# Graph network, four layers: writing the x columns of the wide node rows by DRAM to DRAM transfers ahead of the first node stage

## The reference, cut to what matters

```python
h = jnp.maximum(_layernorm(x), 0.0)
h = h @ W                                   # 128 x 128
deg = segment_sum(ones, src)                # edges and self loops, by source
norm = rsqrt(deg)
agg = segment_sum(h[src] * norm[src], dst) * norm     # self loops included
x = x + tanh(agg / max(l2norm(agg), 1e-12))
```

## Time and profile before

| | |
|---|---|
| median of three runs | 4488.05 us |
| the profiled execution's own time | 4457.76 us |
| its span, first to last instruction | 4456.1 us |
| mean granted TensorE clock | 0.819 of 2.4 GHz |
| node stage, first load to the next stage's first load | 246.0 to 629.4 us |
| prelude, first load to the node stage's first load | 45.1 to 246.0 us |
| DMA traffic of the whole run | 627.73 MB, mean 141 GB/s |
| DMA queues used | SP's (523.79 MB) and GpSimd's (102.76 MB) |

### The profile page before, as it was taken

The page is one execution under the profiler, slowest core; times in us unless marked ns, Lnnn a source line. Parts: engine busy times, 40 slices in busy tenths (PEclk is TensorE's granted clock), DMA queues, the critical chain, the costliest instruction groups (busy, mean ns, idle before and its releaser), DMA issues. The chain is left out here.

```text
span 4456.1 us, 67687 instructions
## 1 busy us (share of the span) xinstructions
PE 3021.5 (68%) x12366; PEld 1720.8 (39%) x12366; DVE 3403.5 (76%) x10033; ACT 2148.5 (48%) x5598; POOL 2108.6 (47%) x2258
## 2 busy tenths in 40 slices
PE   5956644444445999478999124888888999506886
PEld 1255533333332444123444112555545666303443
DVE  6978868888886888675555785888885666597997
ACT  0057766677662222162222265676765666304554
POOL 0057767777775554006553002555545555103566
PEclk9977767777767999689999555898888999758998
DMA  2079966776672222174331596444445556303333
GB/s 51 2 209 285 285 219 219 231 232 227 225 219 87 65 62 59 45 222 86 62 62 42 135 246 157 121 125 121 126 107 180 194 195 199 112 0 110 114 112 87
DMA packets 622136, 627.73 MB, mean 141 GB/s; under 512 B 168453, under 2 KB 495711, under 8 KB 615589
## 3 DMA queue, kind: packets, MB, share of 16 engines
q1 hardware_dynamic: 574020, 523.79, 39.3%
q0 software_dynamic: 48000, 102.76, 9.4%
HBM read 333.97 MB, written 296.91 MB: 142 GB/s over the span
## 5 line engine op out<-in xcount | busy, mean ns | idle before, releaser
L1410 PE MATMUL r_pM<-r_masked,wr 128*128 128x512 f32 x1600 | 747.3, 620 | 55.2 <-DVE r_masked L1361 55.2
L1361 DVE SCALAR_TENSOR_TENSOR r_masked<-r_typ,r_hT 128x512 f32<-128x512 f32 x800 | 493.9, 688 | 238.4 <-ACT r_hT L1388 189.1
L1410 PEld LDWEIGHTS r_pM<-r_masked,wr 128*128 128x128 f32 x1600 | 307.7, 198 | 424.3 <-issue 293.2
L1252 PE MATMUL e_pY<-ident,e_agg 128*128 128x128 f32 x400 | 134.0, 438 | 367.6 <-DVE e_agg L1127 340.3
L741 POOL DMA_INDIRECT q_rows<-nr,row_x x200 | 258.8, 1294 | 193.3 <-PE q_pT L590 132.3
L2408 POOL DMA_INDIRECT out<-o_base,o_at_o x200 | 239.4, 1197 | 165.1 <-DVE o_base L2449 96.8
L741 POOL DMA_INDIRECT r_xs<-h_tab,r_at_s x200 | 214.8, 1074 | 87.7 <-issue 47.0
L741 POOL DMA_INDIRECT r_xs<-tab,r_at_s x200 | 212.4, 1062 | 89.1 <-issue 48.2
L1252 PEld LDWEIGHTS e_pY<-ident,e_agg 128*128 128x128 f32 x400 | 106.9, 327 | 379.5 <-issue 202.4
L590 PE MATMUL g_pT<-ident,g_hT 128*128 128x128 f32 x400 | 95.9, 384 | 226.7 <-ACT g_hT L1772 176.0
L1006 PE MATMUL na_pZ<-w,na_aT 128*128 128x128 f32 x784 | 158.9, 385 | 117.5 <-ACT na_aT L988 117.4
(11 more groups left out here) (402 smaller groups left out, 8958.4 us busy)
## 6 DMA issues: line engine op xcount, KB each, us to landing
xz<-na_xz SPq DMA_DIRECT2D x49, 1040.0 KB, 5.7
r_typ<-vec_s SPq DMA_DIRECT2D x100, 256.0 KB, 3.4
g_al<-alpha_s SPq DMA_DIRECT2D x100, 256.0 KB, 4.3
na_xz<-in_x SPq DMA_DIRECT2D x49, 512.0 KB, 7.0
tab<-na_x SPq DMA_DIRECT2D x49, 512.0 KB
e_xin<-tab SPq DMA_DIRECT2D x49, 512.0 KB, 6.4
hr<-e_hh SPq DMA_DIRECT2D x49, 512.0 KB, 3.8
zh_s<-e_zh SPq DMA_DIRECT2D x49, 512.0 KB, 4.5
```

Source lines behind the costliest of these rows:

```text
L1252: pe.matmul(pY[s][:, cols], agg[s][:, cols], g.ident[:, :], start=True, stop=False)
L1361: v.scalar_tensor_tensor(masked[:, r, :], typ[d.slot(4)][:, :], float(r), hT[d.slot(2)][:, :], ALU.is_equal, ALU.mult).then_inc(ev.mk, 1)
L1410: pe.matmul(pM[s][:, :], g.wr[:, layer * R_ + r, :], masked[:, r, :], start=(r == 0), stop=(r == R_ - 1)).then_inc(ev.mm, 1)
```

## The change

In the prelude ScalarE issues ten transfers from the input x to the first 128 columns of `xz`, both in DRAM, 5,000 rows of 512 bytes each, right behind its table load; it waits for all of them at the end of its prelude work, ahead of the barrier. In the node stage the store of `na_xz` leaves out the x columns and stores 132 of 260 columns.

```diff
-    s_zh, s_cmp, ..., s_out, s_turned = (
-        g.sem("nn_" + n) for n in ("zh", "cmp", ..., "out", "turned"))
-    PER = 8
+    s_zh, s_cmp, ..., s_out, s_turned, s_x = (
+        g.sem("nn_" + n) for n in ("zh", "cmp", ..., "out", "turned", "x"))
+    PER, STRIPS = 8, 10
...
         @block.scalar
         def _(a):
             a.preload_act_table_set("natural_log_exp_and_others")
+            for k in range(STRIPS):
+                strip = slice(k * (N // STRIPS), (k + 1) * (N // STRIPS))
+                a.dma_start(g.xz[strip, 0:P], g.x[strip, :]).then_inc(s_x, 16)
             a.wait_ge(s_deg, 1)
             a.activation(cols[:, 0, :], cols[:, 0, :], ACT.Ln).then_inc(s_norm, 1)
             a.wait_ge(s_norm, 1)
             a.activation(cols[:, 0, :], cols[:, 0, :], ACT.Exp, scale=-0.5).then_inc(s_norm, 1)
+            a.wait_ge(s_x, 16 * STRIPS)
...
-                    sp.dma_start(p.rows(g.xz), xz[p.slot(SLOTS)][:, :, :]).then_inc(w_x[p.slot(SLOTS)], 16)
+                    sp.dma_start(p.rows(g.xz)[:, :, Z_AT:XZ], xz[p.slot(SLOTS)][:, :, Z_AT:XZ]).then_inc(w_x[p.slot(SLOTS)], 16)
```

More of the change, by code:

```diff
@@ L394, in prelude @@
     s_ld, s_z, s_zd, s_big, s_bl, s_pe, s_v, s_d, s_w = (g.sem("wt_" + n) for n in ("ld", "z", "zd", "big", "bl", "pe", "v", "d", "w"))
-    s_zh, s_cmp, s_mm, s_all, s_vec, s_deg, s_norm, s_sum, s_pre, s_row, s_out, s_turned = (
-        g.sem("nn_" + n) for n in ("zh", "cmp", "mm", "all", "vec", "deg", "norm", "sum", "pre", "row", "out", "turned"))
-    PER = 8
+    s_zh, s_cmp, s_mm, s_all, s_vec, s_deg, s_norm, s_sum, s_pre, s_row, s_out, s_turned, s_x = (
+        g.sem("nn_" + n) for n in ("zh", "cmp", "mm", "all", "vec", "deg", "norm", "sum", "pre", "row", "out", "turned", "x"))
+    PER, STRIPS = 8, 10
     with ctx:
```

## The result

| | before | changed |
|---|---|---|
| median of 11 runs each | 4484.96 us | 4504.69 us |
| lowest, highest | 4470.82, 4498.65 | 4491.76, 4519.11 |
| ratio, 95% interval | | 1.0052 [1.0038, 1.0066] |
| span of the profiled execution | 4456.1 us | 4490.0 us |
| prelude, its table load to the node stage's table load | 45.1 to 246.1: 201.0 us | 44.7 to 271.3: 226.6 us |

The changed kernel is slower by half a percent, some 23 us by the ratio (the two medians differ by 19.7), and the prelude alone is 25.6 us longer.

A forecast was written before the change was run, and what follows sets the result against it. The prediction took GpSimd's closed loop to bound the node stage and VectorE, then a short VectorE, ScalarE and TensorE chain, the prelude. Store 0 plus prelude transfers 0 left the median at 4488 us, range 4468 to 4508, chance 0.62.

The forecast's parts named there:

- the 0 for the prelude: Prelude: the ten transfers end at about 210 us, hidden behind VectorE's counting loop, so they cost 0.
- GpSimd's closed loop: Node stage: GpSimd waits only for its own previous steps, 5.45 us of work in 7.47 us a pair, setting the pace.
- the store is worth 0: Node stage: the narrower store takes DMA engines from 98% to some 87% or less; nobody waited for them, so 0.
- the price of a packet: DMA time for one 512-byte packet on one engine: 30.5 ns taken, bounds 20 and 40 ns.
- the cover: Prelude: VectorE's counting loop hides the transfers until 226.6 us for ScalarE's queue, some 240 for the last transfer; 30 us spare.
- The term for company on the engines: Prelude: SP's small loads on the same engines move the transfers' end from 199 to about 210 us.
- rival A: Prelude: DRAM to DRAM packets are dear, 68 ns each, +146 us, 4634 us; half way +66, 4554; chance 0.16.
- Each us past 240 costs one: Prelude: with the cover gone, each us the transfers end after 240 us adds one; at 40 ns a packet, +16 us.
- B: Prelude: SP's small loads are held up while ScalarE's full ring drains, +22 us, 4510 us; chance 0.08.
- C: Node stage: bound by transfers after all, so the narrow store saves 51 us, 4437 us; chance 0.09.
- D: Node stage: the narrow store is dearer than the wide one, 68 ns a packet, +69 us, 4557 us; chance 0.05.
- the budget of a pair: Node stage: 16 DMA engines offer 119.5 engine-us per 7.47 us pair, 117 used; after the change 104, at most 113.

The follow-up runs named there:

- copy-only run: The changed kernel with the node stage's wide store of the kernel before put back, the ten prelude transfers kept: 4482.07 us, ratio 1.0049 to the kernel before.

## Why the prediction was wrong

The forecast was no change, 4488 us, with a range of its own of 4468 to 4508. The median of 4504.69 falls inside, but that is the width of the range and no merit: the ratio of 1.0052 is clear of 1, and the 0 for the prelude was 25.6 us.

**Right.** What bounds the node stage (GpSimd's closed loop, period unchanged, share down, nobody waiting) and that the store is worth 0: the copy alone costs as much as the whole change. The number of engines, 10, and the price of a packet on ten engines, 30.5 ns forecast, 30.1 measured. (Luck has a part in the price: it was taken from transfers on all 16 engines, and on 16 this copy paid 43 ns, so the good end of 95 us with 16 engines did not exist.) The order and size of the cover: Ln needed by 226.6, the final wait by 246.

**Wrong, the step.** "with SP's small loads on the same engines (one of them carries both 97-row loads, some 10 us at 56 to 66) about 210." The term for company on the engines was mis-sized. It counted the 97-row loads and left out the nine strided transfers, although the prediction used just these, at 68 ns each from the earlier trace rows, as the foundation of rival A. Without them the copy was over at 217.5; with them at 269.7. The term of 11 us (210 less 199) was 18 without them and 71 with them. 52 us of this come from the 9,216 four-byte packets, which SP spreads over all 16 engines (without them its queue has 9,360 packets fewer: 9,216, and 16 for each of the nine), 10 of which the copy uses. The loss is mutual: the strided transfers too took 77 us (89.7 to 166.8) in place of 39. The cover of 30 us was gone. "Each us past 240 costs one" comes out somewhat high: 269.7 less 240 is 29.7, while the prelude grew by 25.6; 269.7 less the 246 of the final wait is 24.

**Wrong, a size.** The last transfer was said to land 13.6 us after ScalarE is free; it is 20.8. ScalarE's own lateness and the copy's end come out nearly equal (268 and 271), where I had taken the queue for the stricter of the two.

**The rivals.** A had the right sign and the wrong mechanism: DRAM to DRAM packets of 512 bytes aren't dear, and +146 us did not come. What is dear is their neighbour. B, that SP can't issue beside ScalarE, is refuted: SP's rearranged weights were back by 174 us (issued at 167.24, 6.9 us to land), long before 233.59. Its small part was real, since that was 47 us later than before, but nobody waited for it. C stands refuted, and more than argued: even with GpSimd's loop shortened by 1 us a pair, the wide store is as fast as the narrow. D is refuted by the copy-only run.

**Right for a wrong reason.** I treated 16 x 7.47 = 119.5 engine-us as the budget of a pair and 117 as used. A share of 1.07 shows that this is no budget. The conclusion stood only because GpSimd came first.

The Trainium skill, "DMA: Bandwidth & Descriptors" (Why a DMA increments its semaphore by 16 and not by 1), gave the engine count from the divisors of 5,000. The trace agrees: 10 packets beyond the rows for each transfer of 5,000, and 16 for each of 10,000. The same page (Issuing engines are not separate DMA queues) says that transfers issued from different engines interleave on the same 16; here that meant 32 to 90 GB/s for the copy and SP's transfers together, in place of 170 for the copy alone.

## What to carry to other kernels

Before a transfer is put into an idle stretch, list what else is queued on the same DMA engines there, by packets and not by bytes: a few kilobytes of four-byte elements can hold up megabytes, and a DMA share of 0.18 in that stretch (80 to 119 us) of the kernel before did not warn of it. Ask then for both ends, that of the issuing queue (what stands behind the issues) and that of the last packet (what the barrier waits for), since mending one of two equal ones shows nothing. A high DMA share is no proof of a bound; somebody waiting for a transfer is.

## What the runs showed of the hardware that was not expected

- The DMA share of the profile passes 1: 1.07 at 331 GB/s, 1.34 at 85 GB/s beside the four-byte writes. Packets of one engine overlap, so that a share of 0.98 at 285 GB/s left at least 16% of room.
- A copy from DRAM to DRAM in rows of 512 bytes ran at 170 GB/s on 10 engines, and only at 189 on 16. On 10 it fell further beside small transfers, at a DMA share of 0.34 to 0.40; why is open.
- A queue on ScalarE holds the engine behind it for 204 us of issues; some 19 to 21 us of transfers were outstanding when the last issue ended.
- GpSimd's steps on 128 x 8 numbers took up to 0.5 us longer when they lay beside VectorE's subtraction of 128 x 512 numbers (0.77 in place of 0.25 us, 0.61 in place of 0.20).
